# Two masks of an attention kernel added on TensorE instead of on VectorE

## The chip, the cores and the metric

One core of one Trainium2 chip. The time is that of one execution on the device in microseconds (us), the median of three runs. TensorE (PE in the profile, PEld for its weight loads), VectorE (DVE), ScalarE (ACT), GpSimd (POOL) and the DMA queues (SPq is the one that the sync engine feeds) each work through a fixed order and wait for each other by semaphores.

## The reference

Six attentions of 16 heads (head size 16) run one after the other on a batch of 16 sequences of 256 tokens and 256 features, with layer norms and feed-forward parts between them. In two of the six the scores have a mask over query and key positions before the softmax:

```python
# attention 0 (its mask is one 256 x 256 array, the same for all)
scores = jnp.where(attn_mask == 0, -jnp.inf, scores)
attn = jax.nn.softmax(scores / sqrt(HD), axis=-1)
# attention 2 (causal)
energy = jnp.where(cols[None, :] > cols[:, None], -jnp.inf, energy)
score = jax.nn.softmax(energy / jnp.sqrt(dk), axis=-1)
```

Attentions 1, 3, 4 and 5 have no such mask (0, 2 and 3 have a penalty by key too, which the kernel holds in a row of the keys and which the change leaves alone).

## The kernel before

The unit of work is one sequence in one attention: 96 units, n = 0 to 95, and attention(n) = n // 16. A unit has eight head pairs p. For each pair the scores are computed twice. The step "nat" has queries on the partitions: TensorE fills `ps_nat` (128 x 2 heads x 2 query halves x 256 keys, L566), and VectorE takes the maximum over the keys of each query into `mx` (L1117 to L1135). After four pairs the step "nmt" negates and transposes these maxima, and DMAs place them in a row of the queries. The step "st" runs seven pairs later (LAG = 7): TensorE computes the scores with keys on the partitions into `ps_st` (L581), with the maximum already subtracted through that row; ScalarE takes the exponential of 128 x 1024 values into `pt` (L909); the step "pvg" multiplies by the values (L746).

One `ps_nat` and one `ps_st` exist. So the next nat waits until VectorE has read the maxima of the last (`max_done`, L545), and the next st until ScalarE has read its scores (`exp_done`, L553).

The masks: for `ps_st` TensorE adds them itself, with four bf16 matmuls of an identity and the transposed mask (`st_mask`, L583 to L586; 256 columns each in attention 0, 128 in attention 2). For `ps_nat` VectorE adds them as it takes the maximum: four `tensor_tensor_reduce` for each pair (L1131), of 256 keys each in attention 0, of 128, 256, 128 and 256 in attention 2. Without a mask one `reduce_max` does the whole pair (L1134).

The order of all steps on every engine is one list that a planner sorts by due times written out by hand (`PRE`, `POST`, `plan`). A nat and the st behind it are issued together by `scores`: in attention 0 their matmuls alternate, in later ones the four st matmuls come first and the wait for `max_done` stands between them and the four nat matmuls; the masks of st come last. In between lie the projections, transposes and feed-forward parts of other units ("misc" banks).

Of the kernel before, what the change touches and what calls it, by code (L numbers as in the profile page):

```python
# [214 lines left out]
def block_kernel(nc, t):  # L215
# [3 lines left out]
    with ExitStack() as ctx:  # L219
# [18 lines left out]
        cols = sb("cols", [P, NCOLS])  # L238
        ident = sb("ident", [P, P])
        ident_b = sb("ident_b", [P, P], BF16)  # L240
        causal = sb("causal", [P, 2, P], BF16)
        causal_t = sb("causal_t", [P, P], BF16)
        headsel = sb("headsel", [P, 2 * SLOT])
        iota = sb("iota", [P, S])
# [159 lines left out]
        with nc.Block() as block:  # L404

            @block.sync
            def _(sp):
# [17 lines left out]
                for e in win.order:  # L425
# [21 lines left out]
                    elif kind == "ldt" and n > 0:  # L447

                        wait_filled(sp, ("pvv", n - 2, 0))
                        sp.dma_start(cT[:, rot], t["ctx_t"][u]).then_inc(cT_loaded[rot], 16)  # L450
                        if a == 0:
                            wait_filled(sp, ("pq", n - 2, 1))
                            sp.dma_start(xT[:, rot], t["x_t"][u]).then_inc(xT_loaded[rot], 16)
                    elif kind == "ldn":

                        wait_filled(sp, ("ctr", n - 1 if u else n - 1 - B, 0))
                        if n == 3 * B:
                            wait_filled(sp, ("pk", B - 1, 1))
                            wait_filled(sp, ("pq", B - 1, 1))
                        sp.dma_start(cn[:], t["ctx"][u]).then_inc(cn_loaded, 16)  # L460
                    elif kind == "ldx":
                        if u == B - 3:
                            sp.wait_ge(const_made, 5)
                        sp.dma_start(xn[:, u], t["x"][u]).then_inc(x_loaded[u], 16)
                    elif kind in ("qin", "kin"):
                        if n >= B + 2:
                            sp.wait_ge(st_done, nth(("st", n - 2, 4 * i + 3)))
                        elif n == B and i == 0:
                            sp.wait_ge(rows_in, 64)
                        hi, lo = (part[i:P:2, rot, 0 if kind == "qin" else 1] for part in (upper, lower))  # L470
                        if kind == "qin":
                            wait_out(sp, ("pq", n, 0))
                            dst, parts, done = q_st[:, rot, 4 * i:4 * i + 4].bitcast(F32), (hi, hi, lo), q_in[rot][i]
                            if n == B and i == 0:
                                sp.wait_ge(zeros_made, 2)
                            sp.dma_start(dst[HI_R:P:LO_R - HI_R], zeros[:].unsqueeze(1).to_broadcast([4, 4, S])).then_inc(done, 16)
                        else:
                            wait_out(sp, ("pk", n, 0))
                            dst, parts, done = k_st[:, rot, 4 * i:4 * i + 4].bitcast(F32), (hi, lo, hi), k_in[rot][i]
                        for part, src in enumerate(parts):  # L480
                            sp.dma_start(dst[part:P:STEP], src).then_inc(done, 16)
                    elif kind == "pen" and a == 4:
                        sp.wait_ge(st_done, nth(("st", n - 2, 4 * i + 3)))
                        sp.dma_start(k_st[PEN_R:P:GROUP, rot, 4 * i:4 * i + 4].bitcast(F32),
                                     zeros[0:2].unsqueeze(1).to_broadcast([2, 4, S])).then_inc(pen_in[rot][i], 16)
                    elif kind == "pen" and a == 0:
                        for c in range(2):
                            wait_out(sp, ("pk", n, c))
                        sp.wait_ge(pad_made, 1)
                        sp.dma_start(k[PEN:P:SLOT, n % ROT],  # L490
                                     pen_row[u:u + 1, :].unsqueeze(1).to_broadcast([1, H, S])).then_inc(pad_in[rot], 16)
                    elif kind == "pen":
                        sp.wait_ge(pen_ready, nth(("len", n, 0)))
                        if n >= B + 2:
                            sp.wait_ge(st_done, nth(("st", n - 2, 4 * i + 3)))
                        for m in range(2):
                            sp.dma_start(k_st[PEN_R:P:GROUP, rot, 4 * i + m:4 * i + 4:2].bitcast(F32),
                                         pens[SLOT * m + QUADS * i:SLOT * m + QUADS * i + QUADS]).then_inc(pen_in[rot][i], 16)
                    elif kind == "nmt" and a == 0:
                        sp.wait_ge(shifts_made, nth(e))  # L500
                        row = q[SHIFT:P:SLOT, n % ROT, 2 * i:2 * i + 2, :].rearrange("p c (f b s) -> p b c f s", f=2, b=4)
                        for b in range(4):
                            sp.dma_start(row[:, b], shifts_t[32 * b:32 * b + 16, i, :]).then_inc(shift_in[rot][i], 16)
                    elif kind == "store":
                        wait_out(sp, ("ff2", n, 0))
                        sp.dma_start(t["out"][u], xn[:, u]).then_inc(stored, 16)
# [4 lines left out]
            def _(pe):  # L511
# [16 lines left out]
                def need_nat(e):  # L528

                    _, n, p = e  # L530
                    if p == 0:
                        if n == 0:
                            pe.wait_ge(const_made, 6)
                        if attention(n) == 0:
                            for c in range(2):
                                wait_out(pe, ("pq", n, c))
                                wait_out(pe, ("pk", n, c))
                            pe.wait_ge(pad_in[n % 2], 16 * nth(("pen", n, 0), lambda m, j: m % 2 == n % 2))
                    if attention(n) > 0 and p % 4 == 0:
                        pe.wait_ge(q_in[n % 2][p // 4], placed("qin", n, p // 4))  # L540
                        pe.wait_ge(k_in[n % 2][p // 4], placed("kin", n, p // 4))
                        if ("pen", n, p // 4) in win.place:
                            pe.wait_ge(pen_in[n % 2][p // 4], penned(n, p // 4))
                    if nth(e) > 1:
                        pe.wait_ge(max_done, nth(e) - 1)  # L545
# [9 lines left out]
                def nat_part(e, j, hf):  # L555
# [7 lines left out]
                    else:  # L563
                        lhs = q_st[GROUP * j:GROUP * j + GROUP, n % 2, p, hf * P:(hf + 1) * P]
                        rhs = k_st[GROUP * j:GROUP * j + GROUP, n % 2, p, 0:keys]
                    return nc.tensor.matmul(ps_nat[:, j, hf, 0:keys], lhs, rhs, start=hf == 0, stop=hf == 1)  # L566

                def st_part(e, j, kh):

# [18 lines left out]
                def scores(nat, st):  # L588
# [6 lines left out]
                    for half in range(2):  # L595
# [4 lines left out]
                            if st:  # L600
                                last_st = st_part(st, j, 1 - half if attention(st[1]) == 2 else half)
                        if half == 1:
                            if nat and not apart:
                                last_nat.then_inc(nat_done, 1)
                            if st and attention(st[1]) not in (0, 2):
                                last_st.then_inc(st_done, 1)
                    if nat and apart:
                        need_nat(nat)
                        for half in range(2):
                            for j in range(2):  # L610
                                last_nat = nat_part(nat, j, half)
                        last_nat.then_inc(nat_done, 1)
                    if st and attention(st[1]) in (0, 2):
                        for j in range(2):
# [337 lines left out]
            def _(dve):  # L952
# [46 lines left out]
                for dst, src in ((mask0, xn[:, B - 1]), (mask0_t, xn[:, B - 2])):  # L999
                    nc.vector.tensor_scalar(dst.rearrange("p a b -> p (a b)"), src.rearrange("p a b -> p (a b)").bitcast(I32),  # L1000
                                            0.0, NEG, ALU.is_equal, ALU.mult).then_inc(const_made, 1)
                nc.vector.memset(causal[:, 0, :], 0.0).then_inc(const_made, 1)
                for c, dst in enumerate((causal[:, 1, :], causal_t[:])):
                    nc.vector.tensor_scalar(dst, xn[:, B - 3, 0, c * P:(c + 1) * P], NEG, None, ALU.mult).then_inc(const_made, 1)
                dve.wait_ge(ident_in, 16)
                nc.vector.tensor_copy(ident_b[:], ident[:]).then_inc(const_made, 1)
                for e in win.order:
# [108 lines left out]
                    elif kind == "nat":  # L1116
# [3 lines left out]
                            out = mx[:, i // 4, :].rearrange("p (g c f) -> p g c f", g=4, c=2)[:, g:g + 2, c2, :]  # L1120
                        else:
                            out = mx[:, i // 4, :].rearrange("p (j t f) -> p j t f", j=2, t=4)[:, :, i % 4, :]
                        if a in (0, 2):
                            for j in range(2):
                                for hf in range(2):
                                    if a == 0:
                                        keys, mask = S, mask0[:, hf, :]
                                    else:
                                        keys, mask = (hf + 1) * P, causal[:, 1 - hf:2, :].rearrange("p b s -> p (b s)")
                                    part = ps_nat[:, j, hf, 0:keys]  # L1130
                                    last = nc.vector.tensor_tensor_reduce(part, part, mask, 1.0, FLOOR, ALU.add, ALU.max,  # L1131
                                                                          out[:, j, hf:hf + 1])
                        else:
                            last = nc.vector.reduce_max(out, ps_nat[:], AX)  # L1134
                        last.then_inc(max_done, 1)  # L1135
# [259 lines left out]
```

## Time and profile before

| | |
|---|---|
| median of three runs | 2683.77 us (2679.91 to 2685.1) |
| the profiled execution | 2683.77 us, its span 2682.0 us |
| PE busy | 2483.6 us, 93% |
| DVE busy | 1918.2 us, 72% |
| ACT busy | 1349.6 us, 50% |
| maxima of attention 0 | from 26.6 to 477.6 us of the span |
| maxima of attention 2 | from 988.1 to 1376.9 us |

Matmuls are pipelined: a group of several begins new ones at a closer distance than the duration of one, and a busy PE is not a PE at its peak. Idle time of an engine is shown with what ended it; "issue" is time in which the profile shows nothing that it waited for.

### The profile page before, as it was taken

How to read it: one execution, taken by the hardware profiler on the slowest of the kernel's cores; microseconds unless marked ns; L12 is line 12 of the kernel's file. 1: busy time of each engine (PE TensorE's matmuls, PEld its weight loads, DVE VectorE, ACT ScalarE, POOL GpSimd, SP SyncE). 2: the span in 40 equal slices, each digit the busy share in tenths (PEclk: the TensorE clock that was granted, in tenths of full speed). 3: DMA queues.
4: the chain of work that ended last, by engine and by line, in shares of the span. 5: the costliest groups of instructions: out<-in, count | busy, mean ns of one | idle time of the engine just before them, and what ended most of it. 6: DMA issues, size and time to landing. Idle time of an engine off the chain costs nothing.

```text
span 2682.0 us, 59043 instructions
## 1 busy us (share of the span) xinstructions
PE 2483.6 (93%) x22357; PEld 1869.1 (70%) x22400; DVE 1918.2 (72%) x5500; ACT 1349.6 (50%) x2001; POOL 942.3 (35%) x1158
## 2 busy tenths in 40 slices
PE   6999999999999999888888888889999899999998
PEld 4666666567777778666665666666677668878877
DVE  5788887666666667788877777788788775555552
ACT  0333333444444444455545566666666565555553
POOL 0011111234444443444435555565334332222220
PEclk7999999999999999999999999999999999999999
DMA  3221010121111111222223222112422221111110
GB/s 102 88 63 30 26 35 32 58 80 62 60 58 58 54 57 51 83 76 77 85 81 102 72 75 75 67 65 74 134 87 84 82 72 68 66 66 66 62 62 13
DMA packets 125937, 181.64 MB, mean 68 GB/s; under 512 B 39657, under 2 KB 45977, under 8 KB 125466
## 3 DMA queue, kind: packets, MB, share of 16 engines
q1 hardware_dynamic: 105178, 174.97, 18.9%
q0 software_dynamic: 20480, 2.91, 0.8%
q8 instruction: 181, 2.97, 0.5%
q14 instruction: 98, 0.80, 0.1%
HBM read 40.12 MB, written 4.19 MB: 17 GB/s over the span
## 4 chain that ended last, share of the span: by engine, by line
PE 76%; DVE 13%; ACT 5%; issue 4%; SPq 1%; DMA 1%; POOL 0%; ACTq 0%; DVEq 0%
PE ps_pv L746 12%; PE ps_nat L566 10%; PE ps_st L581 8%; PE ps_misc L842 8%; PE ps_misc L668 6%; PE ps_misc L778 4%; DVE ps_nat L1131 4%; PE ps_misc L705 3%; PE ps_misc L811 3%; ACT pt L909 3%; PE ps_misc L813 2%; PE ps_misc L812 2%; PE ps_misc L757 2%; PE ps_misc L795 2%; PE ps_st L585 2%
## 5 line engine op out<-in xcount | busy, mean ns | idle before, releaser
L909 ACT ACTIVATE pt<-ps_st 128x1024 f32<-128x1024 f32 (+1 forms) x768 | 758.6, 988 | 575.2 <-PE ps_st L585 238.8
L1134 DVE TENSOR_REDUCE mx<-ps_nat 128x4 f32<-128x1024 f32 x512 | 625.6, 1222 | 290.2 <-PE ps_nat L566 289.7
L1255 POOL DMA_DIRECT2D q_st<-shifts_t x640 | 378.8, 597 | 677.0 <-DVE shifts_t L1149 675.9
L581 PE MATMUL ps_st<-q_st,k_st 64*128 64x256 f32 (+1 forms) x2560 | 325.6, 332 | 91.1 <-ACT pt L909 90.6
L746 PE MATMUL ps_pv<-pt,vaug 128*32 128x256 f32 (+1 forms) x6144 | 380.6, 391 | 0.0
L581 PEld LDWEIGHTS ps_st<-q_st,k_st 64*128 64x128 f32 x2560 | 195.4, 187 | 246.2 <-issue 169.4
L1287 POOL TENSOR_TENSOR xn<-xn,tiles 128x512 f32<-128x512 f32 x128 | 163.7, 1279 | 535.0 <-DVE xn L980 293.7
L566 PE MATMUL ps_nat<-k_st,q_st 64*128 64x256 f32 (+1 forms) x2560 | 273.2, 289 | 26.6 <-DVE mx L1134 15.5
L746 PEld LDWEIGHTS ps_pv<-pt,vaug 128*32 128x32 f32 x6144 | 185.6, 114 | 133.9 <-issue 28.1
L1279 POOL TENSOR_TENSOR rstd<-var,half_pow 128x2 f32<-128x2 f32 x144 | 101.6, 709 | 439.0 <-DVE var L976 438.0
L1131 DVE CUSTOM_DVE_ANT_0 ps_nat<-ps_nat,on 128x256 f32<-128x256 f32 x512 | 201.4, 457 | 59.1 <-PE ps_nat L566 58.1
L842 PE MATMUL ps_misc<-weights,hT 128*128 128x256 f32 x1024 | 235.5, 381 | 0.0
L566 PEld LDWEIGHTS ps_nat<-k_st,q_st 64*128 64x128 f32 x2560 | 202.9, 189 | 45.8 <-issue 24.1
L915 ACT ACTIVATE ote<-ps_pv 128x512 f32<-128x512 f32 x192 | 114.8, 598 | 186.7 <-PE ps_pv L746 186.7
L842 PEld LDWEIGHTS ps_misc<-weights,hT 128*128 128x128 f32 x1024 | 189.6, 190 | 25.0
L947 ACT ACTIVATE hT<-ps_misc,cols 128x256 f32<-128x256 f32 x288 | 121.0, 471 | 160.7 <-PE ps_misc L813 130.7
L1131 DVE CUSTOM_DVE_ANT_0 ps_nat<-ps_nat,causal 128x128 f32<-128x128 f32 (+1 forms) x512 | 167.1, 389 | 39.8 <-PE ps_nat L566 39.7
L566 PE MATMUL ps_nat<-qk 17*128 17x256 f32 x1024 | 150.0, 410 | 26.0 <-DVE mx L1131 24.7
L1288 POOL TENSOR_TENSOR xn<-xn,tiles 128x512 f32<-128x512 f32 x128 | 163.9, 1281 | 10.0
L811 PE MATMUL ps_misc<-xF_hi,up_hi 128*128 128x256 f32 x512 | 158.0, 309 | 8.0 <-DVE xF_lo L1051 8.0
L581 PE MATMUL ps_st<-qk 18*128 18x256 f32 x1024 | 149.3, 407 | 0.0
L1131 DVE DVE_READ_ACCUMULATOR2_ANT mx<- 128x1 f32 x1024 | 145.7, 142 | 0.0
(139 smaller groups left out, 4613.4 us busy)
## 6 DMA issues: line engine op xcount, KB each, us to landing
k_st<-qk SPq DMA_DIRECT2D x480, 128.0 KB, 2.1
q_st<-qk SPq DMA_DIRECT2D x480, 128.0 KB
q_st<-shifts_t POOLq DMA_DIRECT2D x640, 4.0 KB, 1.7
weights<-in_weights SPq DMA_DIRECT2D x19, 512.0 KB, 4.4
cT<-in_ctx_t SPq DMA_DIRECT2D x32, 256.0 KB, 2.7
cn<-in_ctx SPq DMA_DIRECT2D x32, 256.0 KB, 2.9
xT<-in_x_t SPq DMA_DIRECT2D x16, 256.0 KB, 3.8
xn<-in_x SPq DMA_DIRECT2D x16, 256.0 KB, 2.8
```

The costliest lines, as they stand in the source:

```text
L566: return nc.tensor.matmul(ps_nat[:, j, hf, 0:keys], lhs, rhs, start=hf == 0, stop=hf == 1)
L581: return nc.tensor.matmul(ps_st[:, j, kh, 0:S - q0], lhs, rhs, start=kh == first, stop=last)
L668: last = nc.tensor.matmul(bank[:, j * S:(j + 1) * S], wv[:, dk, j * P:(j + 1) * P], src[:, dk, :], start=dk == 0, stop=dk == 1)
L746: last = nc.tensor.matmul(ps_pv[32 * j:32 * j + 32, c, q0:S], vaug[:, rot, kh, s, :], pt[:, at_p, s % 2, kh * S:(kh + 1) * S - q0], start= ...
L811: nc.tensor.matmul(out, up_hi[dk][:, cut], xF_hi[:, dk, :], start=dk == 0, stop=False)
L842: last = nc.tensor.matmul(bank[:, th * D:(th + 1) * D], hT[:, ch, th * P:(th + 1) * P], wd[:, ch, :], start=part == 0 and ch == 0, stop=pa ...
L909: nc.scalar.activation(pt[:, g % PT_SLOTS, :, 0:used], ps_st[:].rearrange("p j a b -> p j (a b)")[:, :, 0:used], ACT.Exp, scale=SCALE).the ...
L1131: last = nc.vector.tensor_tensor_reduce(part, part, mask, 1.0, FLOOR, ALU.add, ALU.max, out[:, j, hf:hf + 1])
L1134: last = nc.vector.reduce_max(out, ps_nat[:], AX)
L1255: nc.gpsimd.dma_start(rows[:, b], shifts_t[32 * b:32 * b + 32, i, :]).then_inc(split_in[rot][i], 16)
L1287: link(nc.gpsimd.tensor_tensor(x, x, tile2("g" + name), ALU.mult))
L1288: nc.gpsimd.tensor_tensor(x, x, tile2("b" + name), ALU.add).then_inc(ln_done, 1)
```

## The change

The addition of the mask to `ps_nat` moves from VectorE to TensorE. Behind the nat (and st) matmuls of a pair in attentions 0 and 2, TensorE gets four more bf16 matmuls (`nat_mask`) that add identity times mask to what lies in `ps_nat`; only then is `nat_done` signalled. They stand ahead of the four masks of st. VectorE then takes plain maxima: one `reduce_max` of 128 x 1024 in attention 0; two in attention 2, of 2 x 128 keys for the first query half and 2 x 256 for the second. The tile `causal` loses its half of zeros, and with it one memset at the start.

```diff
-        causal = sb("causal", [P, 2, P], BF16)
+        causal = sb("causal", [P, P], BF16)
...
-                            pe.wait_ge(const_made, 6)
+                            pe.wait_ge(const_made, 5)
...
-                    return nc.tensor.matmul(ps_nat[:, j, hf, 0:keys], lhs, rhs, start=hf == 0, stop=hf == 1)
+                    last = hf == 1 and attention(n) not in (0, 2)
+                    return nc.tensor.matmul(ps_nat[:, j, hf, 0:keys], lhs, rhs, start=hf == 0, stop=last)
+
+                def nat_mask(e, j, hf):
+                    if attention(e[1]) == 0:
+                        return nc.tensor.matmul(ps_nat[:, j, hf, :], ident_b[:], mask0[:, hf, :], start=False, stop=hf == 1)
+                    return nc.tensor.matmul(ps_nat[:, j, hf, hf * P:(hf + 1) * P], ident_b[:], causal[:],
+                                            start=False, stop=hf == 1)
...
-                            if nat and not apart:
+                            if nat and not apart and attention(nat[1]) not in (0, 2):
                                 last_nat.then_inc(nat_done, 1)
...
+                        if attention(nat[1]) != 2:
+                            last_nat.then_inc(nat_done, 1)
+                    if nat and attention(nat[1]) in (0, 2):
+                        for j in range(2):
+                            for hf in range(2):
+                                last_nat = nat_mask(nat, j, hf)
                         last_nat.then_inc(nat_done, 1)
...
-                        if a in (0, 2):
-                            for j in range(2):
-                                for hf in range(2):
-                                    if a == 0:
-                                        keys, mask = S, mask0[:, hf, :]
-                                    else:
-                                        keys, mask = (hf + 1) * P, causal[:, 1 - hf:2, :].rearrange("p b s -> p (b s)")
-                                    part = ps_nat[:, j, hf, 0:keys]
-                                    last = nc.vector.tensor_tensor_reduce(part, part, mask, 1.0, FLOOR, ALU.add, ALU.max,
-                                                                          out[:, j, hf:hf + 1])
+                        if a == 2:
+                            nc.vector.reduce_max(out[:, :, 0], ps_nat[:, :, 0, 0:P], AX)
+                            last = nc.vector.reduce_max(out[:, :, 1], ps_nat[:, :, 1, :], AX)
                         else:
                             last = nc.vector.reduce_max(out, ps_nat[:], AX)
```

## Rows read from the trace of the kernel before

**Rows 1.** The page's first part: busy us (share of the span) xinstructions.

```profile
PE 2483.6 (93%) x22357; PEld 1869.1 (70%) x22400; DVE 1918.2 (72%) x5500; ACT 1349.6 (50%) x2001; POOL 942.3 (35%) x1158
```

**Rows 2.** Busy time by stretch: length, PE, PEld, DVE, ACT, POOL, granted PE clock, DMA share, GB/s.

```profile
26.00:478.00 452.00, 422.64 (x4200) 294.77 (x4243) 355.17 (x1438) 163.97 (x193) 60.20 (x54) 0.97 0.16 46
...
268.00:402.00 134.00, 126.76 (x1327) 88.91 (x1343) 110.28 (x445) 50.77 (x58) 19.85 (x18) 1.00 0.10 31
...
988.00:1377.00 389.00, 350.38 (x3710) 269.98 (x3708) 310.21 (x1506) 186.29 (x282) 158.90 (x201) 0.98 0.22 74
...
1139.00:1340.00 201.00, 174.22 (x2020) 132.09 (x2020) 170.77 (x869) 103.59 (x153) 89.02 (x115) 0.99 0.23 80
```

**Rows 3.** The chain that ended last, shares of 26 to 478 us by line.

```profile
by line: PE ps_nat L566 27.3%; DVE ps_nat L1131 15.4%; PE ps_pv L746 12.5%; PE ps_st L585 9.1%; PE ps_misc L705 6.8%; PE ps_misc L653 6.7%; PE ps_misc L778 5.4%; DVE vT L1100 4.6%; DVE mx L1131 2.8%; issue 2.6%; DVE vaug L1095 2.5%; PE ps_m
```

**Rows 4.** The same chain, shares of 988 to 1377 us.

```profile
by line: PE ps_st L581 9.8%; DVE ps_nat L1131 9.1%; PE ps_nat L566 7.9%; PE ps_st L586 7.4%; PE ps_pv L746 5.7%; PE ps_misc L842 5.3%; ACT pt L909 5.1%; PE ps_misc L661 3.8%; PE ps_misc L662 3.3%; PE ps_misc L663 3.3%; issue 3.1%; SPq L481 
```

**Rows 5.** Waits of PE, 20 to 470 us: total, times, longest us.

```profile
PE ps_nat L566 <- DVE mx L1131: 24.7, 49, 1.7
```

**Rows 6.** Waits of PE, 268 to 402 us.

```profile
PE ps_nat L566 <- DVE mx L1131: 5.9, 15, 0.6
```

**Rows 7.** Waits of PE, 1020 to 1377 us.

```profile
PE ps_st L581 <- ACT pt L909: 26.0, 35, 1.0
PE ps_nat L566 <- DVE mx L1131: 6.5, 15, 1.6
```

**Rows 8.** Timeline of a pair in attention 0: start us, us, engine, line [idle before].

```profile
302.98 0.41 PE L566 MATMUL ps_nat<-qk 17*128 17x256 f32 x2
...
303.33 0.33 PEld L585 LDWEIGHTS ps_st<-on,ident_b 128*128 128x128 bf16 x4 [0.33 <-issue]
303.34 0.61 PE L585 MATMUL ps_st<-on,ident_b 128*128 128x256 bf16 x4
303.43 0.43 DVE L1131 CUSTOM_DVE_ANT_0 ps_nat<-ps_nat,on 128x256 f32<-128x256 f32 x1 [0.75 <-PE ps_nat L566]
...
303.99 1.02 ACT L909 ACTIVATE pt<-ps_st 128x1024 f32<-128x1024 f32 x1 [1.21 <-PE ps_st L585]
...
304.92 0.14 DVE L1131 DVE_READ_ACCUMULATOR2_ANT mx<- 128x1 f32 x1
```

**Rows 9.** Masks of st: ns min/median/max, first and last start us.

```profile
L585 PE MATMUL ps_st<-on,ident_b x512: 272/273/421, 53.8 to 508.7; 128*128 128x256 bf16 x171
...
L586 PE MATMUL ps_st<-causal_t,ident_b x512: 219/219/314, 1016.9 to 1393.8; 128*128 128x128 bf16 x171
```

**Rows 10.** Timeline of attention 2: masks of st, and DVE on one pair.

```profile
1206.24 0.29 DVE L1131 CUSTOM_DVE_ANT_0 ps_nat<-ps_nat,causal 128x128 f32<-128x128 f32 x1
...
1207.46 0.15 DVE L1131 DVE_READ_ACCUMULATOR2_ANT mx<- 128x1 f32 x1
...
1213.80 0.40 PE L586 MATMUL ps_st<-causal_t,ident_b 128*128 128x128 bf16 x4
```

**Rows 11.** Costliest groups: reductions on DVE, busy us, mean ns | idle before.

```profile
L1134 DVE TENSOR_REDUCE mx<-ps_nat 128x4 f32<-128x1024 f32 x512 | 625.6, 1222 | 290.2 <-PE ps_nat L566 289.7
...
L1230 DVE TENSOR_REDUCE tmask<-xn 128x2 f32<-128x512 f32 x32 | 21.7, 680 | 0.0
...
L1086 DVE TENSOR_REDUCE length<-nonzero 128x1 f32<-128x256 f32 x32 | 13.4, 420 | 1.1
```

**Rows 12.** Timeline: two pairs of attention 0 that wait for maxima.

```profile
312.89 0.48 PE L566 MATMUL ps_nat<-qk 17*128 17x256 f32 x2 [0.60 <-DVE mx L1131]
...
314.62 1.02 ACT L909 ACTIVATE pt<-ps_st 128x1024 f32<-128x1024 f32 x1 [2.78 <-PE ps_st L585]
...
315.56 0.14 DVE L1131 DVE_READ_ACCUMULATOR2_ANT mx<- 128x1 f32 x1
...
315.85 0.48 PE L566 MATMUL ps_nat<-qk 17*128 17x256 f32 x2 [0.19 <-DVE mx L1131]
```

**Rows 13.** Pieces of the chain: one group of st masks in each attention.

```profile
303.40 0.54 PE ps_st L585 x4
...
1201.92 0.33 PE ps_st L586 x4
```

More of the change, by code:

```diff
@@ L462, in _ @@
                         if u == B - 3:
-                            sp.wait_ge(const_made, 5)
+                            sp.wait_ge(const_made, 4)
                         sp.dma_start(xn[:, u], t["x"][u]).then_inc(x_loaded[u], 16)
@@ L1001, in _ @@
                                             0.0, NEG, ALU.is_equal, ALU.mult).then_inc(const_made, 1)
-                nc.vector.memset(causal[:, 0, :], 0.0).then_inc(const_made, 1)
-                for c, dst in enumerate((causal[:, 1, :], causal_t[:])):
-                    nc.vector.tensor_scalar(dst, xn[:, B - 3, 0, c * P:(c + 1) * P], NEG, None, ALU.mult).then_inc(const_made, 1)
+                for c, dst in enumerate((causal, causal_t)):
+                    nc.vector.tensor_scalar(dst[:], xn[:, B - 3, 0, c * P:(c + 1) * P], NEG, None, ALU.mult).then_inc(const_made, 1)
                 dve.wait_ge(ident_in, 16)
```

## The prediction

> **What bounds the kernel now.** I read the page first: PE is busy 93% of the span, DVE 72% [rows 1]. The change touches only the stretches of attentions 0 and 2, so I took the busy table for those [rows 2]: 452 us with PE at 94% and DVE at 79%, and 389 us with PE at 90% and DVE at 80%. In the undisturbed middle of attention 2 the two are nearly level, 174.22 and 170.77 of 201 us. PE's granted clock is 0.97 to 1.00, so nearly all of it is at the upper level, 2.4 GHz. Busy shares don't say which engine paces a pair. For that I read the chain of work that ended last. In attention 0 the maxima with their mask (L1131) hold 15.4 + 2.8 = 18.2% of 452 us, 82 us; PE holds most of the rest [rows 3]. In attention 2 they hold at least 9.1%, 35 us [rows 4]. Last, the waits: PE waited for maxima 24.7 us in 450 of attention 0 [rows 5], only 5.9 us in the steady 134 [rows 6], and 6.5 us in attention 2, where it waited 26.0 us for the exponential [rows 7]. So PE paces most pairs, and where DVE is on the chain PE is seldom far behind it.
>
> **What is added on PE.** Four matmuls of bf16 with 256 columns, 128 times (16 units of 8 pairs), and four with 128 columns, 128 times. The masks of st are exactly such operations with the same identity. Four of them last 0.61 us from first start to last end [rows 8], one of them 0.273 [rows 9]: the distance is (0.61 - 0.273) / 3 = 0.112 us, and four more in the same row cost 0.45 us. In attention 2 it is (0.40 - 0.219) / 3 = 0.060 [rows 9, 10], 0.24 us. Total PE work added: 128 x 0.45 = 57.6 us and 128 x 0.24 = 30.7 us, 88 us in all. The 0.33 us of weight-load idle ahead of the st masks [rows 8] is paid once per pair already; the new masks stand ahead of the old ones, so it moves and is not doubled. The bound above: each new group costs its full length, 0.61 us in attention 0 and 0.40 in attention 2 [rows 8, 10]: 78 + 51 = 129 us. The bound below is nothing, where PE waits anyway. I take 0.45 and 0.24, because the new group joins one of its own kind.
>
> The Trainium skill (TensorE: Matmul & The Clock Gate, Back-to-back issue gap) gives about 81 ns per matmul of 128 columns for a sustained stream of load and matmul. By it the groups of attention 2 would cost 0.32 us instead of 0.24, and the sum would rise by 128 x 0.08, an estimated 10 us; the trace here shows 60 ns [rows 9, 10] and I go by it.
>
> **What is removed from DVE.** In attention 0 four operations with their reads of the accumulator run from 303.43 to 304.92 + 0.14 = 305.06, 1.63 us [rows 8]. The one plain maximum of the same 128x1024 took 1.222 us in the other attentions [rows 11]. DVE gains 0.41 us per pair, 52 us in all. In attention 2: 1206.24 to 1207.61, 1.37 us [rows 10], against two plain maxima of 256 and 512 values. The trace has such sizes only from SBUF, 0.420 and 0.680 us [rows 11]; two in a row should overlap a little at their ends, as the four of attention 0 do (0.43 us and more each, and a read of 0.14, in 1.63 us together [rows 8]), so about 1.05 us, an estimate. Bounds: 1.10 (no overlap) and 1222 x 768 / 1024 = 0.92. DVE gains 0.3 us per pair, 38 us in all.
>
> **Where it lands in attention 0.** When DVE does get the scores, it gets them later: before, 303.39 (the last nat matmul, 302.98 + 0.41); after, the four masks begin where the st masks began, 303.34, and end 0.61 later, 303.95. That is 0.56 later, and 0.41 shorter: the maxima are ready 0.15 us later, wherever DVE sat waiting for them. Three kinds of pair:
> - DVE's L1131 chain of 82 us is 50 pairs of 1.63. Ahead of 16 of these, one per unit, stands the transpose of the values (L1100, 4.6% of 452 us, 1.3 each) [rows 3]: DVE is late there and the scores lie ready. Freed DVE time counts, 0.41 us. But PE waited only 0.60 us at such a place [rows 12] and has 0.45 more to do before it: the pair gains at most 0.15, and I count -0.1. Sum -1.6 us.
> - The other 34 go nat, maxima, nat: 312.89 to 315.85, 2.96 us [rows 12]. This ring grows by 0.15 us. But the ring through ScalarE is nearly as long: from 312.89 to the exponential at 314.62, 1.02 us of that, and some 0.15 until the next matmul starts (as behind DVE, from 315.56 + 0.14 to 315.85): 2.90 us [rows 12]. It carries both groups of masks and grows by 0.45 to 3.35. So +0.39 each, 13 us.
> - The remaining 78 pairs are paced by PE (the st masks hold 9.1% of 452 us, 41 us, at 0.54 each some 76 groups [rows 3, 13]): +0.45 each, 35 us.
>
> Together +46 us.
>
> **Where it lands in attention 2.** The st masks hold 7.4% of 389 us, 28.8 us, on the chain at 0.33 each: 87 of 128 groups [rows 4, 13]. The new masks lie on the same stretches, and also where the exponential is waited for (st, nat, both masks, exponential is one ring; it does not hide them): 87 x 0.24 = 21 us. In the other 41 pairs DVE or a transfer is ahead. There PE has 41 x 0.24 = 9.8 us more to do against 6.5 us that it waited for maxima [rows 7], and the maxima come 0.3 us sooner for each queued pair: about +1 us net. Together +22 us.
>
> What hides nothing: POOL, ACT and the transfers have the same work and only start later with PE. One memset fewer and one wait count lower at the start: nothing, the first maxima come at 26.6 us. Attentions 1, 3, 4, 5 keep their instructions.
>
> **The sum** is made against the profiled execution, 2683.77 us with a span of 2682.0, which is also the median: 2683.8 + 46 + 22 = 2752 us, 2.5% slower.
>
> **The rivals.**
> 1. *DVE's relief pays much of it back.* DVE is also on the chain with other work (L1100 and L1095, 7.1% of 452 us, 32 us [rows 3]), and a shorter queue lets each of these start sooner. For it speaks DVE's 80 to 85% in attention 2. Against it: all that PE waited for maxima is 24.7 + 6.5 = 31 us, of which the start-up of attention 0 is a part (steady: 5.9 of 134 us, which makes 20 for the stage). If all 31 vanish and no ring grows, and 10 to 30 us of DVE's 90 come back besides, it is 88 - 31 - 10 to 30 = +27 to +47: 2711 to 2731. With more it goes down to 2695.
> 2. *It is faster: DVE's queue paces the pairs.* If, in the middle of attention 2 above all, the order of waits makes DVE the true bound, each pair gets its 0.41 or 0.30 us back and PE's additions fit into its idle time (389 - 350.4 = 38.6 us, 0.30 us per pair, more than 0.24 [rows 2]). Attention 2 then gains 38 us and attention 0 loses some 10: 2683.8 - 38 + 10 = 2656. It decides at the point where PE's idle time before a nat is longer than the added masks; the rows say 6.5 / 15 = 0.43 us for a wait, but only in 15 of 128 pairs [rows 7], which speaks against it.
> 3. *No change:* the masks take just what DVE gives, 2684.
> 4. *The masks are dearer than their distance*, because a change from small tiles of the array to the whole of it is paid again: up to the 129 us above, 2813; half of that surplus gives 2752 + 20 = 2772 and more. The 81 ns of the Trainium skill (same page and section) lie in this direction, at an estimated +10 us: 2762.
>
> **How the numbers follow.** Forecast (between 2732 and 2780): 0.63. Rival 1: 0.17. Rival 2: 0.09. Rival 3: 0.04. Rival 4: 0.07. The likeliest case gives 2752; leaving out rivals 2 and 3, the lowest part of 1 and the outer part of 4, some 0.2 together, the range is 2704 to 2784. Within 0.2%, 5.4 us, is about what a measurement of this kernel can't tell from no change. Faster 0.09, same 0.05, slower 0.86.
>
> **What would show it.** In attention 0's stretch: DVE's busy time down by about 50 us, PE's up by about 55, the maxima 1.2 us each, 0.5 us later behind the last nat matmul, PE's waits for maxima nearly gone, and units 2.9 us longer each. In attention 2: units 1.4 us longer, the maxima of a pair 1.0 to 1.1 us, the waits for the exponential unchanged in number. Attentions 1, 3, 4 and 5 as long as before. I am wrong if the new masks are not 0.112 and 0.060 us apart, if the stage lengths grow by less than half of 57 and 31 us (rival 1), or if PE's idle time before nat in attention 2 turns out to have been DVE's doing.

## The result, and the profile after

The median went from 2681.84 us (4 runs) to 2727.64 us (4 runs, 2725.37 to 2733.98). The ratio is 1.018, 95% interval 1.0161 to 1.0201: slower by 46 us, where 68 were forecast. (The ratio is taken over more executions, seven of the kernel after; the two medians alone give 1.017.) The sign held, the size was forecast half as large again as it is. The execution that was traced spans 2738.8 us, some 13 us over its median; the part of them that the traces can place, the first unit, is shown below.

The first part of the page after: PE has 80 us more to do [rows 1], DVE 78 us less.

```profile
PE 2564.0 (94%) x23424; PEld 1944.6 (71%) x23424; DVE 1839.7 (67%) x3835; ACT 1349.9 (49%) x2001; POOL 942.9 (34%) x1158
```

The busy table after, over the same steady stretch of attention 0 as in [rows 2] and over eight steady units of attention 2: in attention 0 PE is at 99%.

```profile
268.00:402.00 134.00, 132.71 (x1378) 95.25 (x1377) 87.48 (x158) 46.55 (x54) 18.70 (x17) 1.00 0.10 30
1184.00:1365.00 181.00, 159.20 (x1988) 125.27 (x1986) 132.50 (x354) 87.66 (x129) 74.22 (x97) 1.00 0.22 76
```

The chain after in the stretch of attention 0 (26 to 520 us). The new masks (L571) hold 14.4% of it, DVE's maxima, 18.2% in [rows 3], are no longer in the part that the row shows, and the exponential (L922) has come in:

```profile
by line: PE ps_nat L567 27.7%; PE ps_nat L571 14.4%; PE ps_pv L759 11.3%; PE ps_st L592 10.8%; PE ps_misc L666 10.1%; PE ps_misc L718 6.1%; PE ps_misc L791 4.9%; ACT pt L922 3.4%; PE ps_misc L662 2.5%; PE ps_misc L729 1.8%; PE ps_st L588 1.
```

The waits of PE after, 20 to 510 us. For maxima it waits 2.9 us instead of 24.7 [rows 5]:

```profile
PE ps_nat L567 <- ACT pt L922: 6.1, 16, 1.2
...
PE ps_nat L567 <- DVE mx L1139: 2.9, 5, 1.3
```

A pair of attention 0 in the timeline after, to be set beside [rows 8, 12]. The new masks (0.61) and those of st (0.60) start 0.45 apart; DVE starts when the new masks have ended (342.02) and takes 1.23; the exponential starts 2.16 us behind the start of the pair, where it was 1.73:

```profile
340.34 0.48 PE L567 MATMUL ps_nat<-qk 17*128 17x256 f32 x2
...
341.41 0.61 PE L571 MATMUL ps_nat<-on,ident_b 128*128 128x256 bf16 x4
...
341.86 0.60 PE L592 MATMUL ps_st<-on,ident_b 128*128 128x256 bf16 x4
342.06 1.23 DVE L1139 TENSOR_REDUCE mx<-ps_nat 128x4 f32<-128x1024 f32 x1 [0.74 <-PE ps_nat L571]
...
342.50 1.02 ACT L922 ACTIVATE pt<-ps_st 128x1024 f32<-128x1024 f32 x1 [2.55 <-PE ps_st L592]
...
343.62 0.48 PE L567 MATMUL ps_nat<-qk 17*128 17x256 f32 x2
```

**Unit by unit.** The order of work repeats exactly, so the best ruler is the distance between the first maxima of one unit and of the next. Two such starts in the trace after (units 10 and 11), 30.15 us apart:

```profile
334.71 1.22 DVE L1139 TENSOR_REDUCE mx<-ps_nat 128x4 f32<-128x1024 f32 x1 [2.17 <-PE ps_nat L571]
...
364.86 1.23 DVE L1139 TENSOR_REDUCE mx<-ps_nat 128x4 f32<-128x1024 f32 x1 [2.17 <-PE ps_nat L571]
```

Read so for every unit and every kernel of this study (medians over units 2 to 12 and 37 to 44; within a stretch units of before and after differ from it by at most 0.02 us in attention 0 and 0.25 in attention 2; in the other traces single units of attention 2 stand off by up to 0.6 us, and six units in four traces are 1.1 to 2.2 us longer at a mean granted clock of 0.92 to 0.93). The ratio is to the before of the same session, whose median lay between 2679.0 and 2681.8 us:

```
kernel              median us  ratio to before (95%)     steady unit, us        unit 0
                                                         att. 0     att. 2      us
before              2681.8     1                         27.78      21.16       30.4
after               2727.6     1.018  (1.0161-1.0201)    30.15      22.60       35.5
after_again         2730.5     1.0176 (1.0147-1.0205)    30.15      22.60       29.7
only_0              2714.3     1.0117 (1.0086-1.0148)    30.15      21.14       35.5
only_2              2702.5     1.0083 (1.0061-1.0106)    27.77      22.69       31.3
no_nat_mask         2660.1     0.9932 (0.9911-0.9953)    26.92      21.20       32.9
both_masks          2766.1     1.0319 (1.0294-1.0344)    30.88      23.86       34.3
nat_masks_twice     2804.8     1.0457 (1.0432-1.0481)    33.65      23.93       31.0
st_masks_first      2739.9     1.0220 (1.0190-1.0250)    30.70      22.88       31.3
wide_masks          2728.9     1.0170 (1.0149-1.0192)    30.12      22.59       26.4
fused_before        2680.0     0.9993 (0.9983-1.0004)    27.78      21.13       33.2
fused_after         2724.4     1.0169 (1.0148-1.0191)    30.16      21.97       28.0
fused_no_nat_mask   2646.7     0.9861 (0.9846-0.9876)    26.92      20.21       25.8
one_pair            2674.5     0.9970 (0.9960-0.9981)    27.56      21.16       27.8
```

So the change costs 2.37 us per steady unit of attention 0 (2.9 forecast) and 1.44 of attention 2 (1.4 forecast). The units of the other attentions came out as before.

### The profile page after: what moved, and what is told of

The parts are those of the page before. It is cut to its first block, busy times and chain, and to the rows that moved or that the text cites. A ratio compares the mean times of both kernels' runs of the same rounds, so it can differ in the third digit from the quotient of the medians.

```text
span 2738.8 us, 59469 instructions
## 1 busy us (share of the span) xinstructions
PE 2564.0 (94%) x23424; PEld 1944.6 (71%) x23424; DVE 1839.7 (67%) x3835; ACT 1349.9 (49%) x2001; POOL 942.9 (34%) x1158
## 3 DMA queue, kind: packets, MB, share of 16 engines
q0 software_dynamic: 20480, 2.91, 0.8%
## 4 chain that ended last, share of the span: by engine, by line
PE 80%; DVE 9%; ACT 6%; issue 3%; SPq 1%; DMA 1%; POOL 0%; ACTq 0%; DVEq 0%
PE ps_pv L759 11%; PE ps_nat L567 10%; PE ps_st L588 8%; PE ps_misc L855 8%; PE ps_misc L681 5%; PE ps_misc L791 4%; ACT pt L922 4%; PE ps_misc L718 3%; PE ps_misc L824 3%; PE ps_nat L571 3%; PE ps_misc L770 2%; PE ps_misc L826 2%; PE ps_misc L825 2%; DVE mx L1139 2%; PE ps_st L592 2%
## 5 line engine op out<-in xcount | busy, mean ns | idle before, releaser
L922 ACT ACTIVATE pt<-ps_st 128x1024 f32<-128x1024 f32 (+1 forms) x768 | 758.5, 988 | 633.6 <-PE ps_st L592 277.7
L1139 DVE TENSOR_REDUCE mx<-ps_nat 128x4 f32<-128x1024 f32 x640 | 781.8, 1222 | 411.9 <-PE ps_nat L567 283.7
L759 PE MATMUL ps_pv<-pt,vaug 128*32 128x256 f32 (+1 forms) x6144 | 374.5, 386 | 0.0
L825 PE MATMUL ps_misc<-xF_hi,weights_lo 128*128 128x256 f32 x512 | 145.4, 284 | 0.0
L826 PE MATMUL ps_misc<-xF_lo,up_hi 128*128 128x256 f32 x512 | 145.3, 284 | 0.0
L567 PEld LDWEIGHTS ps_nat<-qk 17*128 17x128 f32 x1024 | 91.6, 190 | 55.6 <-issue 34.0
```

The lines of the kernel that those rows point to most:

```text
L759: last = nc.tensor.matmul(ps_pv[32 * j:32 * j + 32, c, q0:S], vaug[:, rot, kh, s, :], pt[:, at_p, s % 2, kh * S:(kh + 1) * S - q0], start= ...
L825: nc.tensor.matmul(out, lo[:, dk, cut], xF_hi[:, dk, :], start=False, stop=False)
L826: last = nc.tensor.matmul(out, up_hi[dk][:, cut], xF_lo[:, dk, :], start=False, stop=dk == 1)
L922: nc.scalar.activation(pt[:, g % PT_SLOTS, :, 0:used], ps_st[:].rearrange("p j a b -> p j (a b)")[:, :, 0:used], ACT.Exp, scale=SCALE).the ...
```

## The experiments

### The two parts apart

`only_0` and `only_2` make the change in one attention each.

> The change made in attention 0 alone; attention 2 keeps its masks on VectorE. Theory (PE paces, the steady units of attention 0 grew from 27.78 to 30.15 us in the changed kernel): +38 to +40 us against the kernel before, about 2721, and the units of attention 2 stay at 21.16 us. Rival (the two stages share one cause such as the clock or a later slack): less than half of that or more than 50 us.

> The change made in attention 2 alone. Theory: the units of attention 2 grow from 21.16 to 22.60 us, +14 to +20 us over the stage, about 2698; attention 0 stays at 27.78 us per unit. Rival (VectorE really paces attention 2, and the loss there comes from something else): within 5 us of before.

Measured: +35 and +23 us against the before of the same session (2678.96), and each unit length within 0.1 us of where the full change has it, the other attention untouched. In unit lengths the parts add up; the rivals (a common cause, an attention 2 that does not lose) are out. In medians they do so only roughly: 35 + 23 = 58 us, against 46 and 50 for the two sessions of the full change. The median of `only_0` moved a little less than its steady units say (16 x 2.37 = 38), that of `only_2` about as much (16 x 1.53 = 24).

### TensorE's cost and VectorE's relief apart

`no_nat_mask` is the changed kernel without the four matmuls:

```diff
-                    if nat and attention(nat[1]) in (0, 2):
-                        for j in range(2):
-                            for hf in range(2):
-                                last_nat = nat_mask(nat, j, hf)
```

`both_masks` has them and keeps the four `tensor_tensor_reduce` on VectorE.

> The changed kernel without the four added matmuls: nothing adds the mask to the scores of which the maxima are taken, so a query's maximum runs over masked keys too (the scores of the exponential keep their mask). This is VectorE's relief alone. Theory: only the waits for maxima and the place behind the transposes can come back, about 1.3 us per unit in attention 0 and 0.5 in attention 2: -20 to -30 us, about 2657. Rival (VectorE's queue is worth much, my second count of +27 to +47 for the change): -50 us or more, 2630 or less.

> The added matmuls on TensorE, and VectorE still adds its mask too (the mask is added twice to what the maxima are taken of). This is TensorE's cost alone. Theory: 0.44 us in pairs paced by PE, 0.56 in the two per unit that wait for maxima, nothing in the one behind the transposes: +50 in attention 0, and 1.7 us per unit or +28 in attention 2, together about 2760. Rival (the cost of the matmuls is much larger and the relief of VectorE hid it): 2790 or more.

Measured: 2660.1 and 2766.1, close to both expectations (2657 and 2760). By unit they are less close: the relief was expected at 1.3 and 0.5 us and is 0.86 and nothing, and the masks alone were expected to cost 1.7 us in attention 2 and cost 2.70. With before and after they make a table of four, in us per steady unit:

```
                     masks not on PE   masks on PE     cost of the masks
attention 0
 DVE adds masks      27.78             30.88           +3.10
 DVE plain maxima    26.92             30.15           +3.23
 relief              -0.86             -0.73
attention 2
 DVE adds masks      21.16             23.86           +2.70
 DVE plain maxima    21.20             22.60           +1.40
 relief              +0.04             -1.26
```

Attention 0 is as the prediction had it: the masks cost nearly all of 8 x 0.44 = 3.5 us, the relief brings 0.7 to 0.9. Attention 2 is odd. There the relief alone is worth nothing, although DVE is busy 85% [rows 2], and the masks alone cost 2.70 us, more than their own 1.9. The part on the stall in attention 2 finds why.

### The price of one more group, and of one instruction

`nat_masks_twice` issues each new mask twice (the masked scores get twice the penalty); `wide_masks` takes two matmuls of 512 columns for the four of 256 in attention 0.

> The changed kernel with each new mask added twice: eight matmuls instead of four (the masked scores get twice the penalty). Theory: with the waits used up, the next four cost their full distance everywhere, 8 x 0.45 = 3.6 us per unit of attention 0 and 8 x 0.24 = 1.9 of attention 2: +58 and +28, about +85 against the changed kernel, 2813. Rival (there is still slack): less than +60.

> The changed kernel with the masks of nat of attention 0 in two matmuls of 512 columns instead of four of 256. The same columns, half the instructions and weight loads. Theory (columns set the cost): within 3 us of the changed kernel. Rival (each instruction costs a fixed part, or its weight load shows): at least 0.02 us per matmul saved, -5 us or more.

Measured: +3.50 us per unit of attention 0 on top of 30.15, which is 0.437 for each of 8 groups, and +1.33 in attention 2 (1.9 expected). There seven of the eight pairs grew by 0.21 to 0.23 us and the fourth became 0.22 shorter: it is the pair with the stall described below, and PE's 3.0 us of waits for maxima in eight units are gone. In all 2804.8, 74 us over `after_again` in the same session instead of 85. `wide_masks` changed the steady unit by no more than 0.03 us: the columns are the cost, not the instructions.

### The order of the two groups

> The changed kernel with the order of the two groups of masks turned round: those of st first, then the new ones of nat. TensorE's work is the same. Theory of two rings: the exponential gets its scores 0.45 and 0.24 us sooner, the maxima come as much later. Attention 2, where PE waits for the exponential in about three pairs of a unit, gains up to 0.24 us in each, 0.4 to 0.7 us per unit; attention 0 loses in the two or three pairs of a unit in which the ring through the maxima is then 3.5 us long: +0.3 to +0.8 us per unit. Together between -5 and +8 us against the changed kernel. Rival (PE alone paces all pairs): no unit changes by more than 0.1 us.

```diff
-                    if nat and attention(nat[1]) in (0, 2):
-                        for j in range(2):
-                            for hf in range(2):
-                                last_nat = nat_mask(nat, j, hf)
-                        last_nat.then_inc(nat_done, 1)
                     if st and attention(st[1]) in (0, 2):
...
                         last_st.then_inc(st_done, 1)
+                    if nat and attention(nat[1]) in (0, 2):
+                        for j in range(2):
+                            for hf in range(2):
+                                last_nat = nat_mask(nat, j, hf)
+                        last_nat.then_inc(nat_done, 1)
```

Measured: attention 0 +0.55 us per unit, as expected: two pairs wait for the maxima again (0.33 and 0.54 us). Attention 2 was expected to gain 0.4 to 0.7 and lost 0.28. PE's waits for the exponential did fall there (18.8 to 13.4 us in eight units), but the maxima came later and PE waited for them instead (3.0 to 5.7 us). Pair by pair, three became shorter by 0.12 to 0.18 us and four longer by about 0.10, which cancels; the loss lies in the fourth pair, 3.16 to 3.41 us, the one with the stall described below, where DVE's small product takes 1.21 us in most units instead of 0.96. So both rings are real, and which of them is tighter differs from pair to pair. In all the kernel lies 9 us over `after_again`, just outside the expected -5 to +8.

### The second trace of the changed kernel

> The changed kernel itself once more, for a second trace of it. The trace first taken spans 2738.8 us, 11 us over the median, and its first unit is 5.1 us longer than before. Theory (the start-up at half clock varies from run to run): span about 2726, first unit no more than 1 us over the 30.4 of before where the clock rises as early, all steady units again 30.15 and 22.60 us. Rival (the change itself delays the start): the first unit again 35 us.

Measured: a span of 2733.5 us (2726 expected), unit 0 of 29.7 us instead of 35.5, all steady units to the hundredth as before. Over the traces of all kernels unit 0 lies anywhere between 25.8 and 35.5 us. The busy table of 37 to 65 us, after and then `after_again`: the granted clock (the number behind POOL) averages 0.55 and 0.82, so the first was nearly all at 1.2 GHz.

```profile
37.00:65.00 28.00, 25.11 (x117) 15.99 (x114) 9.78 (x13) 4.46 (x5) 0.00 (x0) 0.55 0.11 22
```

```profile
37.00:65.00 28.00, 25.46 (x178) 17.83 (x184) 13.95 (x18) 6.57 (x7) 0.00 (x0) 0.82 0.28 61
```

The longer first unit is not the change's doing. The two traces of the changed kernel and that of its near copy `wide_masks` have first units of 35.5, 29.7 and 26.4 us and spans of 2738.8, 2733.5 and 2729.4 us: the first unit moves the total by some 5 to 10 us, and single spans are poor rulers here.

### The stall in attention 2

The trace of `no_nat_mask` shows where the relief went. Per unit, one pair became 0.45 us shorter (2.91 to 2.46) and a pair further on 0.56 longer (2.72 to 3.28), at a new wait of 0.70 us for maxima. Ahead of these maxima stands a product of 128 x 16 values (L1148), the reciprocals times the pad mask of the queries:

```profile
1240.75 1.27 POOL L1280 TENSOR_TENSOR xn<-xn,tiles 128x512 f32<-128x512 f32 x1
...
1240.97 1.08 DVE L1148 TENSOR_TENSOR rec<-rec,tmask 128x16 f32<-128x16 f32 x1
...
1244.18 0.49 PE L566 MATMUL ps_nat<-k_st,q_st 64*128 64x128 f32 x4 [0.70 <-DVE mx L1124]
```

In the kernel before, between two additions on POOL, with the next nat at 1255.69 (start us, us, engine):

```profile
1251.75 1.29 POOL L1287 TENSOR_TENSOR xn<-xn,tiles 128x512 f32<-128x512 f32 x1 [3.94 <-ACT xn L920]
...
1252.97 0.39 PE L566 MATMUL ps_nat<-k_st,q_st 64*128 64x128 f32 x4
1253.03 0.17 DVE L1156 TENSOR_TENSOR rec<-rec,tmask 128x16 f32<-128x16 f32 x1
1253.11 1.28 POOL L1288 TENSOR_TENSOR xn<-xn,tiles 128x512 f32<-128x512 f32 x1
...
1255.69 0.50 PE L566 MATMUL ps_nat<-k_st,q_st 64*128 64x128 f32 x4
```

In the kernel after, at the same place:

```profile
1303.78 1.28 POOL L1292 TENSOR_TENSOR xn<-xn,tiles 128x512 f32<-128x512 f32 x1 [4.33 <-ACT xn L933]
...
1305.14 1.28 POOL L1293 TENSOR_TENSOR xn<-xn,tiles 128x512 f32<-128x512 f32 x1
...
1305.42 0.39 PE L567 MATMUL ps_nat<-k_st,q_st 64*128 64x128 f32 x4
1305.48 0.96 DVE L1161 TENSOR_TENSOR rec<-rec,tmask 128x16 f32<-128x16 f32 x1
...
1308.58 0.50 PE L567 MATMUL ps_nat<-k_st,q_st 64*128 64x128 f32 x4 [0.35 <-DVE mx L1137]
```

The reader is to see the ends: POOL's second addition ends at 1306.42, DVE's tiny product at 1306.44. Before, the product started where the first addition ended (1253.04), ahead of the second (1253.11), and took 0.17 us; after, it starts 0.34 us into the second and lasts as long as that. This is so throughout: in the eleven traces that have the product, all 114 that took more than 0.3 us ended 0.03 to 0.04 us behind the end of such an addition. It also explains the cost of 2.70 us in `both_masks`: the product takes 1.13 to 1.16 us there, and of the 2.70 us 0.96 lie in the fourth pair, the one in which it stands. The busy time of this one line over eight steady units, before (16 products), then after:

```profile
1139.00:1309.00 170.00, 2.80 (x16) 1.00 0.23 81
```

```profile
1184.00:1365.00 181.00, 9.19 (x16) 1.00 0.22 76
```

That fits a rule of the Trainium skill (SBUF — State Buffer, SBUF: two separate sides): VectorE and GpSimd share a pair of ports, and a VectorE operation with two inputs in SBUF and a GpSimd operation that reads SBUF do not run together; whichever starts first holds the ports to its end. To test whether the stall is what attention 2 paid for, I folded the product into the one behind it, which reads PSUM, so that each operation there has one of its two tensors in PSUM:

```diff
-                            m = tmask[:, u, a - 2, :].unsqueeze(2).to_broadcast([P, 2, H // 2])
-                            link(nc.vector.tensor_tensor(rec[:, i], rec[:, i], m, ALU.mult))
...
+                            for hf in range(2):
+                                last = nc.vector.scalar_tensor_tensor(dst[:, hf, 8 * i:8 * i + 8, :], src[:, hf],
+                                                                      tmask[:, u, a - 2, hf:hf + 1], by[:, hf],
+                                                                      op0=ALU.mult, op1=ALU.mult)
```

> The changed kernel with the small product of the reciprocals and the pad mask (128x16, two operands in SBUF) folded into the two products behind it, which read PSUM. In the changed kernel that small product took 0.96 us instead of 0.17 once per unit of attention 2, while GpSimd added the layer norm's bias. Theory (the shift of the work by the change brought the two on top of each other, and part of what attention 2 lost is that stall): DVE's stall is gone, the pair behind it grows by 0.24 instead of 0.44 us, the steady unit of attention 2 goes from 22.60 to about 22.3 us, 3 to 6 us less over the stage. Rival (the stall lies beside other work): the unit stays at 22.60.

> The same fold in the kernel before, where the small product took 1 us in only two or three units of attention 2. Theory: nothing to gain, 21.16 us per steady unit stays within 0.1 us, the time within 0.2% of before. Rival (the fold itself saves VectorE time that counts, or the two products of 128 are dearer): a change of more than 0.2 us per unit.

> No mask on the scores of which the maxima are taken (they run over masked keys too), and the fold. Without the fold VectorE's relief gave nothing in attention 2 (21.20 us per steady unit against 21.16), since PE gained 0.45 us at one pair and lost 0.56 at another, behind a small product of 1.08 us. Theory: with the stall gone the relief comes through, about 20.6 us per unit, 5 to 9 us over the stage, total about 2653. Rival (PE and the exponential pace attention 2 anyway): 21.1 us per unit, total 2660.

Measured: the steady unit of attention 2 stayed where it was in the kernel before (21.16 and 21.13), and fell from 22.60 to 21.97 in the changed one and from 21.20 to 20.21 in `no_nat_mask`, 0.63 and 0.99 us where 0.3 and 0.6 were expected. The kernel before has no such stall in its steady units, and there the fold gains nothing. (The wait for the mask, `msk_done`, stands at the same place with and without the fold, so it is not what was removed.) The same place in `fused_after`, POOL's second addition and DVE's products side by side, and the next nat without a wait:

```profile
1288.11 1.28 POOL L1297 TENSOR_TENSOR xn<-xn,tiles 128x512 f32<-128x512 f32 x1
1288.15 0.26 DVE L1157 RECIPROCAL rec<-ps_misc 128x16 f32<-128x16 f32 x1 [1.11 <-PE ps_misc L770]
...
1288.38 0.39 PE L567 MATMUL ps_nat<-k_st,q_st 64*128 64x128 f32 x4
1288.45 0.61 DVE L1173 SCALAR_TENSOR_TENSOR on<-ps_misc,tmask,rec 128x128 f32<-128x128 f32 x2
...
1291.03 0.39 PE L567 MATMUL ps_nat<-k_st,q_st 64*128 64x128 f32 x4
```

Of the totals, `fused_no_nat_mask` shows it clearly (2660.1 to 2646.7). For `fused_after` the 3 to 6 us that it lies below the two medians of the changed kernel are within their scatter; there the claim rests on the unit lengths, and on the length of the whole stage of attention 2 in the traces, 396.7 us against 408.2 and 410.3. With the fold the three cells of attention 2 that I have make sense: relief 21.13 to 20.21, -0.92 us; masks 20.21 to 21.97, +1.76 us, which is 0.22 for each of eight pairs. The fourth cell, masks on both engines with the fold, was not run.

### One pair only

`one_pair` moves to TensorE only the mask of the second pair of each unit of attention 0, 16 groups in all.

> The kernel before with the masks of one pair per unit of attention 0 moved to TensorE, the pair behind the transposes of the values (p = 1), 16 pairs in all; all others stay on VectorE. Theory: it is the only kind of pair that gained in the changed kernel (3.80 to 3.28 us... the interval of that pair, where its neighbour grew), here 0.2 to 0.4 us per unit: 27.4 to 27.6 us, -3 to -6 us in all, at the edge of what can be measured. Rival (TensorE's 0.45 us shows there too): 27.9 us or more.

Measured: 0.997 (0.9960 to 0.9981), 27.56 us per unit, 0.22 less; that pair went from 3.80 to 3.57 us and its wait of 0.60 is gone. (The 3.28 in the expectation is the neighbour's; in the changed kernel this pair takes 3.58.) It computes what the kernel before does and is the fastest such version here. `fused_no_nat_mask`, 1.4% faster than before, leaves the mask out of the maxima, so its softmax subtracts a maximum that may belong to a masked key; that is good only while no row's masked scores lie far above its others.

## Why the prediction was right, and where its size was off

**What bounds the kernel: right.** PE paces most pairs of attention 0. Doubling the new work cost its full price there, 0.437 us for each group.

**What is added: right.** 0.45 and 0.24 us per group were forecast. Measured in attention 0 are 0.43 to 0.44 for each pair paced by PE, and the groups start 0.45 apart. In attention 2, with the stall removed, they are 0.19 to 0.24 for each pair. The upper bound of 129 us for dearer masks is out (rival 4), and so are the 81 ns per matmul of 128 columns that the prediction took from the Trainium skill (TensorE: Matmul & The Clock Gate, Back-to-back issue gap): in the trace after the four new masks and the four of st start 0.23 us apart, 58 ns per matmul.

```profile
1300.44 0.40 PE L572 MATMUL ps_nat<-causal,ident_b 128*128 128x128 bf16 x4
...
1300.67 0.39 PE L593 MATMUL ps_st<-causal_t,ident_b 128*128 128x128 bf16 x4
```

**What is removed: right.** 1.23 us instead of 1.63 in attention 0. In attention 2 the two maxima take 0.43 + 0.68 us, from first start to last end 1.02 (1303.05 to 1304.07), against 1.05 forecast:

```profile
1303.05 0.43 DVE L1136 TENSOR_REDUCE mx<-ps_nat 128x2 f32<-128x256 f32 x1 [0.49 <-PE ps_nat L572]
...
1303.39 0.68 DVE L1137 TENSOR_REDUCE mx<-ps_nat 128x2 f32<-128x512 f32 x1
```

**Where it lands in attention 0: the term that was too large.** 46 us were forecast (the three terms as written add up to 46.8); 16 x 2.37 is 38, and the stage as a whole, start-up included, grew by 31 and 39 us in the two traces. Pair by pair in a steady unit (distance of the starts of nat, us):

```
before           3.35  3.80  2.96  3.48  4.43  2.96  3.32  3.48
no_nat_mask      3.35  3.39  2.85  3.48  4.43  2.80  3.14  3.48
after            3.78  3.58  3.28  3.92  4.86  3.24  3.57  3.92
forecast change  +0.45 -0.10 +0.39 +0.45 +0.45 +0.39 +0.45 +0.45
measured change  +0.43 -0.22 +0.32 +0.44 +0.43 +0.28 +0.25 +0.44
```

The three kinds of pair are there. Mis-sized were the 78 pairs "paced by PE": four of eight per unit are, 64 in all; the fifth (3.32) had 0.18 us to gain from a faster DVE, which the count of st masks on the chain cannot show. The two ring pairs grew by 0.30 and not 0.39, since they too had 0.11 and 0.16 of DVE in them; and the pair behind the transposes gained 0.22, not 0.1. Together 2.93 us per unit were forecast and 2.37 measured. The ring through ScalarE was named rightly: the 2.96 that became 3.24 now shows a wait of 0.24 for the exponential. Its length was put 0.1 us too high, 2.90: in `no_nat_mask`, where the same pair has the same wait of 0.24, it is 2.80, and 2.80 + 0.44 = 3.24.

**Where it lands in attention 2: right in size, for a wrong reason.** 1.44 us per unit came out as forecast. But in it are +1.76 for the masks, -0.92 of relief, where I had counted 41 pairs nearly even, and +0.63 for a stall that I did not foresee. The two errors cancelled, which is luck.

**The total.** 68 forecast, 46 measured: about 8 of the difference lie in the steady units of attention 0. The steady lengths alone would make 16 x (2.37 + 1.44) = 61 us, and the stages of both attentions grew by 31 + 20 and 39 + 18 us in the two traces. So some 15 us between the steady units and the medians remain open: the units at either end of a stage, the start-up and the clock differ from run to run, and I cannot divide it further.

**The rivals.** *DVE's relief pays much back* holds for a part. It put the time at 2711 to 2731, and 2728 is inside, while the forecast's own interval began at 2732. Of the 8 x 0.44 = 3.5 us of new work in a unit of attention 0 1.15 were not paid, where the forecast left out 0.67; in attention 2 the relief is worth 0.92 us once the stall is gone, where the forecast counted almost nothing. *Faster* is out: DVE paces neither stage, since even without any mask work on PE the relief gives only 0.7%, or 1.4% with the stall removed. Its condition held in one pair of 8, and `one_pair` made a gain of it. *No change* is out: the ratio's interval begins at 1.0161.

## What to carry to other kernels

Work moved from an engine that is 80% busy to one that is 94% busy costs its full price in every pair that the second engine paces and returns only the waits that lie on the path: per steady unit of attention 0 3.1 us were paid and 0.7 got back. Where a pair shows a wait longer than the work to be moved, move it there alone: 16 of 256 groups gave 0.3% where all of them lost 1.8%. When relief of a busy engine brings nothing, compare the durations of the same small instructions in both traces; a shift of half a microsecond can lay two engines on top of each other.

## What the runs showed of the hardware that was not expected

- A VectorE product of 128 x 16 values from SBUF takes 0.17 us alone. Where it started during GpSimd's addition of 128 x 512 values in SBUF it ended with that addition: 0.96 us in after, 1.08 in `no_nat_mask`, 0.74 to 1.22 in the steady units of the other kernels that stalled there. It was not delayed where it started during GpSimd's product of 128 x 2 values, recorded at 0.71 us: 0.17 to 0.18 us, three times in the trace after. The products with one operand in PSUM that took its place in `fused_after` were never delayed: 0.34 to 0.35 us each, all 128 of them.
- The first unit took 25.8 to 35.5 us in fourteen traces of nearly the same start. From 37 to 65 us PE's granted clock averaged 0.55 and 0.57 in after and `only_0` (35.5 us each), 0.82 in `after_again` (29.7) and 0.94 in `wide_masks` (26.4). The order is not strict: a clock of 0.70 went with 27.8 us in `one_pair`, 30.4 in before and 34.3 in `both_masks`. What sets it off at one level or the other was not tried.
- Two bf16 matmuls of 512 columns cost what four of 256 do: 30.12 against 30.15 us per unit.
